# A light expert padded to full shape, a 64 KB weight load ahead of x, and values moved between two key blocks

## The reference

```
x1 = layernorm(x  + self_attention(x))            # 16 heads of 64, biases on q, k, v, out
x2 = layernorm(x1 + cross_attention(x1, ctx))     # attends over the 16 heads at each position
y  = layernorm(x2 + ffn(x2))
ffn(x): light = gelu(rms_norm(x) @ w1_light + b1) @ w2_light + b2     # inner width 64
        heavy = the same with its own weights                          # inner width 512
        all 128 tokens of each sequence are chosen for heavy, so both are added
```

## Time and profile before

| | |
|---|---|
| median of three timed runs | 410.6 us (410.17 to 410.63) |
| the profiled execution | 410.04 us |
| its span from first to last instruction | 408.2 us |
| TensorE busy | 397.0 us (97%) |
| VectorE, ScalarE, GpSimd busy | 286.8, 240.2, 147.7 us |
| mean granted clock of TensorE | 0.998 of full speed |

### The profile page before, as it was taken

One profiled execution on the slowest core, in us unless ns is written; L12 is line 12 of the kernel. 1 busy time (PEld: TensorE's weight loads), 2 busy tenths in 40 slices (PEclk: granted clock), 3 DMA queues, 4 the chain that ended last, 5 costly groups with the idle time before them and its releaser, 6 DMA issues.

```text
span 408.2 us, 15943 instructions
## 1 busy us (share of the span) xinstructions
PE 397.0 (97%) x6580; PEld 342.8 (84%) x6580; DVE 286.8 (70%) x661; ACT 240.2 (59%) x813; POOL 147.7 (36%) x224
## 2 busy tenths in 40 slices
PE   7999899999999999999999999999999999999995
PEld 6788788888888888788988888888988888888874
DVE  4593786965857787866849678677747878677545
ACT  4686654844756584745567465655567566547350
POOL 1540543431523354431413454323315445323223
PEclk9999999999999999999999999999999999999999
DMA  7900112210110213110110213100201110210001
GB/s 267 359 4 8 35 29 53 77 40 2 28 35 10 46 26 86 43 29 8 32 25 16 47 32 88 39 16 10 45 11 27 42 37 19 51 38 21 27 26 53
DMA packets 43646, 19.27 MB, mean 47 GB/s; under 512 B 36592, under 2 KB 40944, under 8 KB 43584
## 3 DMA queue, kind: packets, MB, share of 16 engines
q1 hardware_dynamic: 42592, 16.62, 15.8%
q0 software_dynamic: 560, 1.38, 0.9%
q10 hardware_dynamic: 432, 0.34, 0.3%
HBM read 8.88 MB, written 1.05 MB: 24 GB/s over the span
## 4 chain that ended last, share of the span: by engine, by line
PE 86%; DVE 5%; SPq 3%; DMA 2%; issue 2%; ACT 1%; POOL 0%; POOLq 0%; ACTq 0%; DVEq 0%
PE ps L1226 7%; PE ps L1171 7%; PE ps L1047 7%; PE ps L1075 7%; PE ps L1130 7%; PE ps L1151 7%; PE ps L1139 6%; PE ps L1027 5%; PE ps L1029 4%; PE ps L1028 4%; PE ps L1181 4%; PE ps L1066 4%; PE ps L1106 3%; SPq L314 3%; PE ps L1165 2%; PE ps L1159 2%
## 5 line engine op out<-in xcount | busy, mean ns | idle before, releaser
L541 ACT ACTIVATE p<-ps,neg_max 128x128 f32<-128x128 f32 x256 | 90.3, 385 | 40.7 <-DVE neg_max L810 40.7
L411 POOL TENSOR_TENSOR p<-p,row_inv 128x1024 f32<-128x1024 f32 x32 | 60.7, 1898 | 61.9 <-DVE row_inv L816 61.9
L534 ACT ACTIVATE pt<-ps 128x512 f32<-128x512 f32 x62 | 34.4, 626 | 47.9 <-PE ps L1130 47.9
L541 ACT ACTIVATION_READ_ACCUMULATOR p<-ps,neg_max 128x1 f32 x256 | 57.8, 226 | 0.0
L810 DVE TENSOR_REDUCE neg_max<-ps 128x4 f32<-128x512 f32 x64 | 41.5, 672 | 4.8 <-PE ps L1226 4.0
L756 DVE TENSOR_TENSOR ot<-ps,bv 128x512 f32<-128x512 f32 x32 | 22.0, 688 | 29.7 <-PE ps L1151 29.5
L1130 PE MATMUL ps<-ident,p 128*128 128x128 f32 x256 | 34.7, 279 | 1.7 <-issue 0.9
L1226 PE MATMUL ps<-kt,qt 64*64 64x128 f32 x1024 | 35.2, 275 | 0.0
L1139 PE MATMUL ps<-x1t,wq 128*64 128x64 f32 x1024 | 33.5, 224 | 0.9 <-DVE v2s L766 0.9
L1139 PEld LDWEIGHTS ps<-x1t,wq 128*64 128x64 f32 x1024 | 31.3, 138 | 2.2 <-issue 1.1
L1171 PE MATMUL ps<-wo,ot 128*128 128x128 f32 x256 | 32.7, 281 | 0.5 <-DVE ot L756 0.5
(11 more groups left out here) (159 smaller groups left out, 837.1 us busy)
## 6 DMA issues: line engine op xcount, KB each, us to landing
v<-v2s SPq DMA_DIRECT2D x256, 32.0 KB
xg<-x_t SPq DMA_DIRECT2D x4, 256.0 KB, 3.6
cg<-ctx_t SPq DMA_DIRECT2D x4, 256.0 KB, 3.7
wo<-w_o SPq DMA_DIRECT2D x2, 512.0 KB, 9.2
xres<-x_nat SPq DMA_DIRECT2D x15, 64.0 KB, 1.7
pt<-w_qk SPq DMA_DIRECT2D x3, 256.0 KB, 5.2
out<-x2b SPq DMA_DIRECT2D x3, 256.0 KB, 2.3
x2b<-w_v SPq DMA_DIRECT2D x1, 512.0 KB, 6.3
```

The costliest lines, as they stand in the source:

```text
L411: nc.gpsimd.tensor_tensor(ph, ph, row_inv[:, 8 * half:8 * half + 8].unsqueeze(2).to_broadcast([T, 8, T]), ALU.mult).then_inc(p_ready, 1)
L534: nc.scalar.activation(pt[:, u * BANK:(u + 1) * BANK], bank(T_BANK[u]), ACT.Copy).then_inc(pt_ready, 1)
L541: last = nc.scalar.activation(p[:, hd * T:(hd + 1) * T], bank(S_BANK[q])[:, pos * T:(pos + 1) * T], ACT.Exp, bias=neg_max[:, hd:hd + 1], a ...
```

## The change

The light chunk is padded with zeros to 128 columns in `up` and 128 rows in `down`; its weights are part of `w_up` and `w_down`, and `wdl` and its load go. The first piece of `w_qk` is cut into 128 and 384 columns; SP's queue loads the 128 columns (64 KB) first, then x, then the 384; ScalarE's queue begins with the bias. The 128 columns are split ahead of x, and the bias is scaled between. In unit 0 lo·hi goes ahead of hi·lo. In step 0 `values(0)` stands between E and F on TensorE, and `values_out` directly behind the exponentials on ScalarE.

```diff
+FP = NF * 128
-        wup_hi, wup_lo = (sb("wup_" + part, [128, FH + FL], fp32r) for part in ("hi", "lo"))
-        wdn = sb("wdn", [128, (NF - 1) * D])
-        wdl = sb("wdl", [FL, D])
+        wup_hi, wup_lo = (sb("wup_" + part, [128, FP], fp32r) for part in ("hi", "lo"))
+        wdn = sb("wdn", [128, NF * D])
...
-        SPLITS = ([(wqk, wqk_hi, wqk_lo, u, in_wqk[u]) for u in range(4)] + ...
-        WQK_SPLIT, WV_SPLIT, WV2_SPLIT = [1, 2, 3, 4], 6, 8
+        QK_PARTS = [slice(0, 128), slice(128, BANK)] + [slice(u * BANK, (u + 1) * BANK) for u in range(1, 4)]
+        HALVES = [slice(0, BANK), slice(BANK, 2 * BANK)]
+        SPLITS = ([(wqk, wqk_hi, wqk_lo, cols, loaded) for cols, loaded in zip(QK_PARTS, in_wqk)] + ...
+        WQK_SPLIT, WV_SPLIT, WV2_SPLIT = [2, 3, 4, 5], 7, 9
...
# SP's queue
-            sp.dma_start(xg[:], x_t[0]).then_inc(in_xg, 16)
-            for u in range(1, 4):
-                sp.dma_start(wqk[:, u * BANK:(u + 1) * BANK], w_qk[:, u * BANK:(u + 1) * BANK]).then_inc(in_wqk[u], 16)
+            for n, cols in enumerate(QK_PARTS):
+                sp.dma_start(wqk[:, cols], w_qk[:, cols]).then_inc(in_wqk[n], 16)
+                if n == 0:
+                    sp.dma_start(xg[:], x_t[0]).then_inc(in_xg, 16)
...
# GpSimd's queue: one load fewer
-                              (wdn[:], w_down), (wdl[:], w_down_light), (bup[:], b_up)):
+                              (wdn[:], w_down), (bup[:], b_up)):
...
# ScalarE
-            act.dma_start(wqk[:, 0:BANK], w_qk[:, 0:BANK]).then_inc(in_wqk[0], 16)
             act.dma_start(bqk[:], b_qk).then_inc(in_bqk, 16)
...
+                    split_hi(0)
                     x_high(0)
-                    split_hi(0)
                     split_hi(1)
                     split_hi(2)
+                    split_hi(3)
                     act.wait_ge(bq_scaled, 1)
                     qk_out(0, "A", FIRST_BANKS)
-                    split_hi(3)
+                    split_hi(4)
                     qk_out(0, "B")
...
                     exponentials(3)
                 if static and s == 0:
+                    values_out(0, 0)
                     c_high(0)
-                    split_hi(6)
                     split_hi(7)
-                    values_out(0, 0)
+                    split_hi(8)
...
# VectorE
-            dve.wait_ge(in_bqk, 16)
-            nc.vector.tensor_scalar(bqk[:, 0:NC], bqk[:, 0:NC], DH ** -0.5, None, ALU.mult).then_inc(bq_scaled, 1)
-            dve.wait_ge(bq_scaled, 1)
...
                 if static and s == 0:
+                    split_lo(0)
+                    dve.wait_ge(in_bqk, 16)
+                    nc.vector.tensor_scalar(bqk[:, 0:NC], bqk[:, 0:NC], DH ** -0.5, None, ALU.mult).then_inc(bq_scaled, 1)
                     x_low(0)
-                    split_lo(0)
+                    dve.wait_ge(bq_scaled, 1)
                     split_lo(1)
                     split_lo(2)
+                    split_lo(3)
                     qk_out(0, "A", FIRST_BANKS)
-                    split_lo(3)
+                    split_lo(4)
                     qk_out(0, "B")
...
-                    nc.vector.tensor_scalar(wup[:, FH:FH + FL], wup[:, FH:FH + FL], gam[:, 0:1], ...
+                    nc.vector.tensor_scalar(wup[:, FH:FP], wup[:, FH:FP], gam[:, 0:1], ...
...
# TensorE
-                product3(bank(H_BANK[n])[0:m, :], wup_hi[:, cols], wup_lo[:, cols],
+                product3(bank(H_BANK[n]), wup_hi[:, cols], wup_lo[:, cols],
...
-                    w = wdn[:, c * D:(c + 1) * D] if c < NF - 1 else wdl[:]
-                    last = nc.tensor.matmul(bank(Y_BANK[g])[:, bb * D:(bb + 1) * D], ht[g % 2][c][0:m, bb * T:(bb + 1) * T], w,
+                    last = nc.tensor.matmul(bank(Y_BANK[g])[:, bb * D:(bb + 1) * D], ht[g % 2][c][:, bb * T:(bb + 1) * T],
+                                            wdn[:, c * D:(c + 1) * D],
...
                     pe.wait_ge(x_hi, 1)
-                    pe.wait_ge(w_hi, WQK_SPLIT[0])
+                    pe.wait_ge(w_hi, 1)
                     nc.tensor.matmul(bank(FIRST_BANKS[0]), wqk_hi[:, 0:128], xg_hi[:], start=True, stop=False)
+                    pe.wait_ge(w_lo, 1)
+                    nc.tensor.matmul(bank(FIRST_BANKS[0]), wqk_lo[:, 0:128], xg_hi[:], start=False, stop=False)
                     pe.wait_ge(x_lo, 1)
-                    nc.tensor.matmul(bank(FIRST_BANKS[0]), wqk_hi[:, 0:128], xg_lo[:], start=False, stop=False)
+                    nc.tensor.matmul(bank(FIRST_BANKS[0]), wqk_hi[:, 0:128], xg_lo[:], start=False, stop=True).then_inc(mm_qk, 1)
                     pe.wait_ge(w_lo, WQK_SPLIT[0])
-                    nc.tensor.matmul(bank(FIRST_BANKS[0]), wqk_lo[:, 0:128], xg_hi[:], start=False, stop=True).then_inc(mm_qk, 1)
...
                     project_k2(0, "E", lambda r: None)
-                    project_k2(0, "F", lambda r: read_k2(r, "E"))
                     pe.wait_ge(exp_ready, 2)
                     pe.wait_ge(w_lo, WV_SPLIT)
                     values(0)
+                    project_k2(0, "F", lambda r: read_k2(r, "E"))
                     pe.wait_ge(in_ident, 16)
```

More of the change, by code:

```diff
@@ L51, in build @@
           w2_q, w2_k, w2_v, w2_o, b2_q, b2_k, b2_v, b2_o,
-          w_up, g_light, g_heavy, w_down, w_down_light, b_up, bd_light, bd_heavy,
+          w_up, g_light, g_heavy, w_down, b_up, bd_light, bd_heavy,
           ident_in, perm_in, mask_in, own_j_in, out):
@@ L155, in build @@
         wqk, wv, wv2 = pt, x2b, v2
-        wup = x2b[:, (B - 5) * D:(B - 5) * D + FH + FL]
+        wup = x2b[:, (B - 5) * D:(B - 5) * D + FP]
         fx_hi, fx_lo = [xg_hi, cg_hi], [xg_lo, cg_lo]
@@ L210, in build @@
         in_xg, in_cg = sem("in_xg"), sem("in_cg")
-        in_wqk = [sem(f"in_wqk{i}") for i in range(4)]
+        in_wqk = [sem(f"in_wqk{i}") for i in range(5)]
         in_bqk = sem("in_bqk")
@@ L279, in looped @@
             return not isinstance(s, int) or FIRST_LOOPED <= s <= LAST_LOOPED
-        SPLITS = ([(wqk, wqk_hi, wqk_lo, u, in_wqk[u]) for u in range(4)] + [(wv, wv_hi, wv_lo, u, in_wv) for u in range(2)] +
-                  [(wv2, wv2_hi, wv2_lo, u, in_wv2) for u in range(2)])
-        WQK_SPLIT, WV_SPLIT, WV2_SPLIT = [1, 2, 3, 4], 6, 8
+        QK_PARTS = [slice(0, 128), slice(128, BANK)] + [slice(u * BANK, (u + 1) * BANK) for u in range(1, 4)]
+        HALVES = [slice(0, BANK), slice(BANK, 2 * BANK)]
+        SPLITS = ([(wqk, wqk_hi, wqk_lo, cols, loaded) for cols, loaded in zip(QK_PARTS, in_wqk)] +
+                  [(wv, wv_hi, wv_lo, cols, in_wv) for cols in HALVES] + [(wv2, wv2_hi, wv2_lo, cols, in_wv2) for cols in HALVES])
+        WQK_SPLIT, WV_SPLIT, WV2_SPLIT = [2, 3, 4, 5], 7, 9
         @block.sync
         def _(sp):
-            sp.dma_start(xg[:], x_t[0]).then_inc(in_xg, 16)
-            for u in range(1, 4):
-                sp.dma_start(wqk[:, u * BANK:(u + 1) * BANK], w_qk[:, u * BANK:(u + 1) * BANK]).then_inc(in_wqk[u], 16)
+            for n, cols in enumerate(QK_PARTS):
+                sp.dma_start(wqk[:, cols], w_qk[:, cols]).then_inc(in_wqk[n], 16)
+                if n == 0:
+                    sp.dma_start(xg[:], x_t[0]).then_inc(in_xg, 16)
             sp.dma_start(wv[:, 0:HD], w_v).then_inc(in_wv, 16)
@@ L417, in step @@
                 if isinstance(s, int) and s == 1:
-                    pool.wait_ge(in_ffn, 8 * 16)
+                    pool.wait_ge(in_ffn, 7 * 16)
                     nc.gpsimd.tensor_tensor(bdl_row[:], bdl_row[:], bdh_row[:], ALU.add).then_inc(bd_summed, 1)
@@ L454, in split_hi @@
             def split_hi(n):
-                tile, hi, _, u, loaded = SPLITS[n]
+                tile, hi, _, cols, loaded = SPLITS[n]
                 act.wait_ge(loaded, 16)
-                nc.scalar.activation(hi[:, u * BANK:(u + 1) * BANK], tile[:, u * BANK:(u + 1) * BANK], ACT.Copy).then_inc(w_hi, 1)
+                nc.scalar.activation(hi[:, cols], tile[:, cols], ACT.Copy).then_inc(w_hi, 1)
             def x_high(group):
@@ L522, in gelu @@
                 g, c = n // NF, n % NF
-                m = 128 if c < NF - 1 else FL
                 act.wait_ge(mm_h, n + 1)
-                nc.scalar.activation(ht[g % 2][c][0:m, :], bank(H_BANK[n])[0:m, :], ACT.Gelu,
-                                     bias=bup[0:m, c:c + 1]).then_inc(ht_ready, 1)
+                nc.scalar.activation(ht[g % 2][c], bank(H_BANK[n]), ACT.Gelu, bias=bup[:, c:c + 1]).then_inc(ht_ready, 1)
             def step(s, h, g, phase, a, bc, d):
@@ L574, in step @@
                 if static and s == 0:
-                    split_hi(4)
                     split_hi(5)
+                    split_hi(6)
                 if phase == 1 and a and not static:
@@ L625, in _ @@
             exp2(B)
-            act.wait_ge(in_ffn, 8 * 16)
+            act.wait_ge(in_ffn, 7 * 16)
             gelu(0)
@@ L659, in _ @@
             nc.vector.memset(warm[:], 0.0).then_inc(warm_set, 1)
-            dve.wait_ge(in_bqk, 16)
```

(31 more changed lines are left out.)

## The result

The changed kernel takes 407.25 us (median of four runs, 406.35 to 407.5) against 410.38 (410.08 to 410.63) for the kernel before: a ratio of 0.992, interval 0.9902 to 0.9938, which is 2.5 to 4.0 us. It is faster by 3.1 us; the forecast was 406.2 and a gain of 4.4. The profiled execution took 407.05 us (span 405.2, clock 0.998), 2.99 less than the one before.

What follows compares the result with a forecast made beforehand. TensorE was taken as the bound, 86% of the span's last-ending chain. Terms 1.57 + 0.49 - 0.19 + 2.54 = 4.41 us turned the profiled 410.04 into 405.6; the median forecast was 406.2, likeliest 405.4 to 407.2, range 405.0 to 408.2.

Steps and rivals of the forecast that it cites:

- rival 1: Start: x lands no earlier (5.33), so the start gives about 0.5 us; total 407.3 us; chance 0.12.
- start, to E: Front of the kernel: reordered loads and earlier splits gain 1.57 us, bounds 0.5 and 1.9.
- values between E and F: Step 0: values moved between the key blocks remove TensorE's 0.73 wait, gaining 0.49 us; bounds 0.1 and 0.73.
- wup preparation: Step 1: splitting 640 columns instead of 576 on VectorE's path loses 0.19 us, bounds 0.1 and 0.3.
- tail: Feed-forward end: full chunks replacing 64-row ones in down gain 2.54 us, bounds 1.9 and 2.75.
- the 1.35: Start: the part of the gain from unit 1 counting as 6.72 against 8.07.
- the forecast's 6.50: Start: time in us at which unit 1 was to begin on TensorE.
- C's stall: Start of block C: the 0.22 us stall at 12.97 goes too, with nothing to spare.
- 2 (the place, not the rows): Tail: light chunk's 0.39 comes from its place, waiting for a gelu, so tail stays; 408.7 us; chance 0.07.
- 3 (drain in `up`): Light ups also pay a tiling-mode drain, so padding gives 1.6 us more; 404.8 us; chance 0.06.
- 4: No effect: front and tail gains are both taken back, say by loop transfers; 410.6 us; chance 0.04.
- 5: Slower: stop-and-go products at the start drop TensorE's clock to its lower level; up to 415 us; chance 0.05.

Runs made afterwards that it cites:

- experiment 4: The changed kernel measured again, unedited: 406.68 us, ratio 0.9901 to the kernel before.
- experiment 5: Changed kernel with the 384-column weight piece loaded on ScalarE's queue behind the bias instead of SP's: 406.41 us, ratio 0.9909 to the kernel before.
- experiment 6: As experiment 5, with the fourth weight piece (columns 1024 to 1536) on ScalarE's queue too: 406.92 us, ratio 0.9921 to the kernel before.
- experiment 7: As experiment 6, with 9 products on zeros instead of 12: 407.21 us, ratio 0.9926 to the kernel before.
- experiment 2: Kernel before with the start edits alone (64 KB weights first, x second, bias first on ScalarE's queue, unit 0): 409.54 us, ratio 0.9983.
- Experiment 11: As Experiment 10, with 9 products on zeros instead of 12: 406.71 us, ratio 0.9898 to the kernel before.
- experiment 12: Kernel before with one edit, the bias loaded first on ScalarE's queue, ahead of its 256 KB of weights: 409.8 us, ratio 0.9977.
- Experiment 10: Changed kernel with VectorE reading block A ahead of the fourth split and B ahead of the fifth: 406.09 us, ratio 0.9904 to the kernel before.
- experiment 8: Changed kernel with the light chunk padded in down only, up back at 64 columns: 406.93 us, ratio 0.9919 to the kernel before.
- experiment 9: Changed kernel with the light chunk padded in up only, down reading 64 rows: 409.02 us, ratio 0.9954 to the kernel before.

## Why the prediction was right, and where it was off

The chain was the forecast one: start, values and tail each gave time on TensorE, and of what they gave only the pause and the loop's 0.20 were lost again. All three big terms lay in their bounds, but most errors went the same way. The time alone would have misled: 407.25 is the number of rival 1 (407.3), whose mechanism did not occur. Part of the shortfall may be spread between measurements: the same kernel in experiment 4 gained 3.6 by the medians and 4.1 by the ratio.

Forecast and trace, in us; the last column is what the profiled execution lost or gained on the forecast:

| term | forecast | measured | difference |
|---|---|---|---|
| start, to E | 1.57 | 0.88 | -0.69 |
| values between E and F | 0.49 | 0.63 | +0.14 |
| wup preparation | -0.19 | -0.10 | +0.09 |
| loop, to 366 us | 0 | -0.20 | -0.20 |
| pause in the short products, light `up` behind them | 0 | -0.56 | -0.56 |
| tail | 2.54 | 2.34 | -0.20 |
| sum | 4.41 | 2.99 | -1.42 |

**Start: the step that failed.** "ScalarE's 384-column split runs beside x_low" took the piece as there. I had worked out when x lands, and it came 0.3 earlier than that, but for the loads behind it I had written only that they have the same bytes ahead of them as before. The 384 columns landed at 5.66, after x_high had ended at 4.87, and unit 1 began at 6.92 for 6.50, its first product 0.50 for 0.45. Of the 1.35, 0.88 came. Experiments 4 to 7 show that this is no single cause that can be taken away: with the piece early, the zeros' end or x was late, and E stayed between 19.75 and 20.19. In experiment 2 x, the piece and unit 1 were early, and the last weight piece, landing at 10.16, held C. Experiment 11 shows in one execution that the forecast's 6.50 is there when the zeros, x and the 384 columns are all early; E came at 19.41 even so, for the forecast's 20.75 - 1.57 = 19.18. Which of the start's three edits gave the 0.88 stays open (experiment 12).

**C's stall.** "... the 0.22 stall at 12.97 goes too, with nothing to spare." It did not go. VectorE's reading of B stands behind the last weight split, this behind ScalarE's split (9.92) and that behind ScalarE's readings of A, which follow unit 1: an earlier start moves both sides. The forecast's margin was 0.05, too thin to count on. In experiment 2 the same split waited for its load instead. Experiment 10 takes the split from ahead of the reading, and the stall goes.

**Values.** Right, and a little better: three changes of tile form were priced at 0.20 each. The row at 23.52 (0.43) shows the one into the values; F's 64 products take 3.64, as E's (3.65), where half of 7.15 is 3.58, and the transposes 1.90 where I had 1.98. GpSimd's second half ends at 28.96, in time.

**Preparation.** The subtraction takes 0.82 for 0.76, as worked out; the copy takes the 0.65 that it took for 576 columns. 0.10 was the lower bound.

**Tail.** Mechanism right, as experiments 8 and 9 show from both sides. The size was off by 0.20: the last group takes 4.63, while 40 x 0.111 is 4.45. My 1.38 for it was 1.20. The trace shows most of the difference: the passes start every 0.11, but each is listed with 0.27 from start to end, so the group ends 0.16 behind 40 x 0.111. The 5.83 held that end too; I had left it out on one side only. The rest is the first light chunk, which gave 0.34 for 0.39: transposes stand behind it (0.22 for 0.37), not a product. That VectorE ends as late as TensorE held.

**The pause.** Not in the forecast. In the first profiled execution of the changed kernel the 64 short products at 366 us lost 0.51, in the second 0.26, in the kernels of the other experiments nothing there; experiments 7 and 11 lost 0.6 and 1.1 near 196 us. The trace names no releaser ("issue"). The place repeats: both executions of the changed kernel paused in one group, and both kernels with 9 products on zeros after the 48th product of one group (7 paused once more, by 0.4, near 149). But experiments 5, 6 and 10, whose TensorE instructions are those of the changed kernel, show no pause at 366. Whether the change brings it stays open, and so does its cause. The remaining 0.05 is the light `up` behind those products: its first product takes 0.43 where it took 0.38, and 0.38 again in experiment 8, so here padding `up` costs 0.05.

**Rivals.** 1 (x late) falls by the 4.24, though another load took x's part and the size that it gave the start, 0.5, is nearer to 0.88 than mine. 2 (the place, not the rows) falls by experiment 9, 3 (drain in `up`) by 8, 4 and 5 by the time. One chunk's 1.16 (at 387.76) stays in all kernels and was there before (389.16); no run shows what it waits for. The loop's 0.20 comes in steps of under 0.1 and is not explained.

## What to carry to other kernels

Where a narrower operand runs between full ones, look at the first product behind it: 0.43 for 0.23 in the row behind a 64-row chunk named a price that padding with zeros removed, while the same look at the 64-column products of `up` said that there was nothing to gain. When a load is moved ahead of another, work out the landing of every load behind it as carefully as its own; here the critical wait went from the bias to a weight piece, moving that to another queue gave it to x, and with both early it went once to the last weight piece. And a stall whose two sides both follow the same start doesn't go when the start is moved; it goes when the order between them is changed.

## What the runs showed of the hardware

The 24 passes on zeros take 4.40 to 5.49 us in different executions of the same instructions. In the slowest (experiment 12) they go at 0.22 each to the end; in the quickest (the changed kernel's first profile) the listed length of a pass falls from 0.42 to 0.27 before they end, and full passes in the tail go at 0.111. The ratio of two is that of TensorE's levels (1.2 and 2.4 GHz), but the granted clock says 1.00 in these stretches throughout, so that the clock is the cause is not shown. With 9 products instead of 12 the first real product took 0.79 once and 0.50 another time.

From 6 to 7 us the one queue of the changed kernel moved 223 GB/s, two queues 402 (experiment 6). Over all kernels with the new start, one queue moved 221 to 293 in that stretch (seven executions), two queues 332 to 402 (three, experiments 5 to 7). DMA: Bandwidth & Descriptors of the Trainium skill, section Issuing engines are not separate DMA queues, says that a second issuing engine saves only the issue time. In total time the runs agree, since no split over queues gained anything; in the rate of that stretch they don't. The transfers in flight differ too, and no run separates that from the number of queues.
